# Layer 1's short chunk of a CIN tower as two fp32r passes over stacked high and low rows

## The chip, the cores and the metric

The kernel runs on one core of one Trainium2 chip. The metric is the device time of one launch in microseconds, from the program's start to its end. The core has five engines that run their own instruction streams and meet at semaphores: TensorE (PE in the profile, with its weight loads as PEld), VectorE (DVE), ScalarE (ACT), GpSimd (POOL) and SyncE (SP), which here only issues DMAs. ScalarE and GpSimd issue DMAs too.

## The reference

The model is a recommendation tower: 39 embedding tables, three cross layers (CIN), and a small MLP. For each of 1024 samples the 39 rows of 16 numbers are looked up (`x0`), and each cross layer multiplies every field of `x0` with every row of the layer before and sums the products with a filter:

```
x0 = xk = e                       # (1024, 39, 16)
for W in (f0, f1, f2):            # (39*39, 128), (128*39, 128), (128*39, 128)
    z = einsum('bfd,bgd->bfgd', x0, xk).reshape(b, f * g, d)
    cur = einsum('bpd,pm->bmd', z, W)
    outs.append(cur); xk = cur
z = sum(concatenate(outs, axis=1), axis=-1)          # (1024, 384)
h = concatenate([z, dense_ctx], axis=1)              # (1024, 400)
y = relu(relu(h @ W_top1 + b_top1) @ W_top2 + b_top2) @ W_top3
```

All inputs are fp32.

## The kernel before, in words

Columns are pairs of sample and embedding dimension, so there are 1024 x 16 of them. They are worked off in 32 groups of 512 columns (`GCOLS`), each of 4 tiles of 128 columns; 4 groups are a batch of 128 samples, and there are 8 batches. The counter `u` in the code counts tiles within a batch.

Layer 1 uses the symmetry of x0 times x0: a pair of fields is met once, by its cyclic distance. With 39 fields there are 20 distances (0 to 19). A chunk holds three distances (`SPT`), that is 117 rows (`KR`), and there are 7 chunks (`KT`): chunk k has the distances k, k+7 and k+14. Chunk 6 would have 6, 13 and 20, and since distance 20 is not needed its last 39 rows are weighted with zero. One chunk of one group is: the second factor moved into `prods[:, k]` by SyncE (`move_second`, line 272), a multiplication with the first factor in PSUM on VectorE (`multiply`, line 789), and matmuls that add into one PSUM bank (`cin1`, line 479).

A chunk is summed in one of two ways. A plain chunk (k = 0, 4, 5, 6) is one fp32 matmul, which the profile shows as two records. A split chunk (k = 1, 2, 3) has its products split: ScalarE rounds them to fp32r (`split_high`, line 654), VectorE takes what is left (`split_low`, line 795), and TensorE makes three fp32r passes: high by high, low weight by high, high weight by low.

Layer 2 is most of the work. For each tile its 39 filter slices are 10 PSUM bank loads (`BANKS`) of four slices (the last of three), each of three fp32r passes of 512 columns (lines 499, 500, 503). The banks go round a ring of 5 (`RING`): TensorE may write bank load n only when load n-5 has been read. Loads 0, 3, 5 and 7 of a tile are read by ScalarE (`scale`, line 670), loads 1, 2, 4, 6, 8 and 9 by VectorE (`mac`, line 823); both multiply by the field's scalar, and GpSimd adds up (lines 417, 421). VectorE's first sum of a tile needs ScalarE's load 0 of that tile. Layer 3 is rearranged into a small matmul per tile (line 515) and 39 per batch (line 526).

Layer 1 of the next group runs beside layer 2 of this one. The place of each of its steps is written out by hand: a pair (tile, q) in a table means "behind bank load q of that tile of the group", and each engine puts the step there in its own stream. In `PRODUCTS`, `HIGHS`, `LOWS` and `CIN1` the n-th pair is the place of the n-th product, split or chunk. In group 1 all places come three loads later (`LATE`). Group 0 runs in a prologue, all of it in fp32. SyncE works its DMAs off in order: for each group the rows to DRAM and back (lines 250, 259), first factors (266), eight moves of the scalars (326), then the second factors of the next group (272), each when `s_cin1` says that the chunk before it has been summed.

Of the kernel before, what the change touches and what calls it, by code (L numbers as in the profile page):

```python
# [26 lines left out]
F32 = mybir.dt.float32  # L27
# [6 lines left out]
P = 128  # L34
# [36 lines left out]
SPLIT = (1, 2, 3)  # L71
NS = len(SPLIT)

# [39 lines left out]
def pair_rows():  # L113

    k, i, f = np.ogrid[:KT, :SPT, :F]
    g, h = (f - KT * i) % F, (f + k) % F
    apart = KT * i + k + 0 * f
    return g * F + h, h * F + g, apart


def cin_tower(nc, dense_ctx, ids, first_row, tables, w_top1, b_top1, w_top2, b_top2, w_top3,
              w0_pair, w0_mirror, f1, f2, c_mask, c_eye, rows, out):
    with ExitStack() as ctx:
# [23 lines left out]
        prods_low = sb("prods_low", [KR, NS, GCOLS], F32R)  # L147
        x1_high = sb("x1_high", [P, 2, GCOLS], F32R)
# [16 lines left out]
        dense_rows = sb("dense_rows", [P, NBATCH, ROWS3])  # L165
# [5 lines left out]

        h1 = terms_flat[:, 0:2 * H1 // P * 512].rearrange("p (h c n) -> p h c n", h=2, c=H1 // P)
# [27 lines left out]
        s_prod = sem("products_ready")  # L200
        s_high = sem("product_highs_ready")
# [67 lines left out]
        def move_second(queue, k, j):  # L269

            at = j % GROUPS * GCOLS
            queue.dma_start(prods[0:KR, k, :], x0_cols[k:k + KR, at:at + GCOLS]).then_inc(s_second[k - 1], 16)  # L272
# [21 lines left out]
        def _(sp):  # L294
# [34 lines left out]
            def move_seconds(gf, j):  # L329

                for k in range(1, KT):
                    sp.wait_ge(s_cin1, gf * KT - KT + k + 1)
                    move_second(sp, k, j)
# [26 lines left out]
            next_cols(1, 1)  # L360
            move_seconds(1, 1)
# [89 lines left out]
        def _(pe):  # L451
# [14 lines left out]
            def cin1(gf, k, first=False):  # L466

                if k == 0:
                    pe.wait_ge(s_scal, gf + 1)
                if k in SPLIT and not first:  # L470
                    i = SPLIT.index(k)
                    pe.wait_ge(s_low, gf * NS - NS + i + 1)
                    passes = ((w0_high[:, i, :], prods_high[:, i, :]), (w0_low[:, i, :], prods_high[:, i, :]),
                              (w0_high[:, i, :], prods_low[:, i, :]))
# [3 lines left out]
                for n, (w, x) in enumerate(passes):  # L478
                    mm = nc.tensor.matmul(ps[:, X1_BANK, :], w, x, start=(k == 0 and n == 0),  # L479
                                          stop=(k == KT - 1 and n == len(passes) - 1))  # L480
# [50 lines left out]
            def prologue():  # L531
# [13 lines left out]
                for k in range(KT):  # L545
                    cin1(0, k, True)
                pe.wait_ge(s_w0h, NS)
                pe.wait_ge(s_w0l, NS)
# [370 lines left out]
```

## Time and profile before

| | before |
|---|---|
| median of 3 runs | 1282.36 us (1281.91 to 1282.44) |
| the profiled execution | 1282.15 us |
| its span, first to last instruction | 1280.3 us |
| PE busy | 1247.0 us, 97% |
| DVE busy | 1038.5 us, 81% |
| POOL busy | 951.5 us, 74% |
| ACT busy | 751.1 us, 59% |
| TensorE clock granted | 1.000 |
| DMA engines busy (queue q1 / q10) | 20.4% / 0.4% |

The busy time of an engine is the time in which any of its instructions ran. Matmuls overlap in the records: a pass of 512 columns is shown as 388 to 454 ns long, while passes start 0.23 us apart. What one costs is therefore read from the distance of starts or from the chain of work, not from the mean length. 1.85 us of the profiled execution lie outside its span.

### The profile page before, as it was taken

What the parts mean: (1) busy time and instruction counts of PE and PEld (TensorE: products, weight loads), DVE (VectorE), ACT (ScalarE), POOL (GpSimd) and SP (SyncE); (2) the same over time, 40 slices, a digit from 0 to 9 for tenths busy, and PEclk for the clock granted to TensorE, in tenths of its full rate; (3) what the DMA queues carried; (4) which work ended last, traced back from release to release, by engine and by line L of the source; (5) the groups of instructions that cost most, each with busy time, mean ns of one, the idle gap of its engine ahead of it and who ended that gap; (6) DMA issues with size and microseconds to landing.
All of it is one profiled execution on the core that took longest, in us unless ns stands there. A gap on an engine that the chain in (4) does not pass through costs nothing.

```text
span 1280.3 us, 19891 instructions
## 1 busy us (share of the span) xinstructions
PE 1247.0 (97%) x5493; PEld 963.6 (75%) x5493; DVE 1038.5 (81%) x3346; ACT 751.1 (59%) x2422; POOL 951.5 (74%) x844
## 2 busy tenths in 40 slices
PE   1999999999999999999999999999999999999999
PEld 0677778777787778777787777877787777877765
DVE  4789896898868996889969888699978898788830
ACT  4456664666646665666646666466656666466641
POOL 6578886788868886788868888588867888675640
PEclk9999999999999999999999999999999999999999
DMA  7632222122212221122221222222221222111000
GB/s 174 180 102 61 66 69 61 45 54 68 62 57 69 68 60 40 50 61 68 69 54 38 68 61 66 61 68 61 53 48 51 66 69 68 47 44 50 1 1 1
DMA packets 121764, 78.69 MB, mean 61 GB/s; under 512 B 77436, under 2 KB 89826, under 8 KB 121652
## 3 DMA queue, kind: packets, MB, share of 16 engines
q1 hardware_dynamic: 107418, 73.69, 20.4%
q0 software_dynamic: 10240, 2.64, 2.4%
q10 hardware_dynamic: 3994, 1.09, 0.4%
q8 instruction: 44, 0.72, 0.2%
q14 instruction: 68, 0.56, 0.1%
HBM read 18.50 MB, written 2.63 MB: 16 GB/s over the span
## 4 chain that ended last, share of the span: by engine, by line
PE 97%; DMA 1%; POOL 1%; issue 0%; ACTq 0%; ACT 0%; DVE 0%; SPq 0%
PE ps L499 23%; PE ps L503 22%; PE ps L500 22%; PE ps L479 14%; PE ps L526 6%; PE ps L515 5%; PE ps L582 2%; PE ps L592 1%; PE ps L462 1%; POOL x_in L393 1%; DMA x_in<-in_tables,row_at 0%; PE ps L599 0%; ACTq L272 0%; DMA x_rows<-x_in 0%; DMA ids_now<-in_ids 0%
## 5 line engine op out<-in xcount | busy, mean ns | idle before, releaser
L823 DVE SCALAR_TENSOR_TENSOR terms<-ps,x_scal,terms 128x128 f32<-128x128 f32 x2944 | 805.7, 341 | 158.4 <-ACT terms L670 94.5
L670 ACT ACTIVATE terms<-ps,x_scal 128x128 f32<-128x128 f32 x2048 | 585.3, 369 | 370.4 <-PE ps L503 363.6
L417 POOL TENSOR_TENSOR terms<-terms 128x1024 f32<-128x1024 f32 (+2 forms) x384 | 577.4, 1504 | 178.5 <-DVE terms L823 156.3
L499 PE MATMUL ps<-w_high,x_high 128*128 128x512 f32 (+1 forms) x1280 | 581.7, 454 | 2.9 <-DVE x_low L801 2.9
L503 PE MATMUL ps<-w_high,x_low 128*128 128x512 f32 (+1 forms) x1280 | 496.1, 388 | 0.0
L500 PE MATMUL ps<-w_low,x_high 128*128 128x512 f32 (+1 forms) x1280 | 494.3, 386 | 0.0
L393 POOL DMA_INDIRECT x_in<-in_tables,row_at x320 | 305.2, 954 | 81.5 <-issue 65.1
L499 PEld LDWEIGHTS ps<-w_high,x_high 128*128 128x128 f32 x1280 | 240.6, 188 | 82.9 <-issue 20.6
L500 PEld LDWEIGHTS ps<-w_low,x_high 128*128 128x128 f32 x1280 | 241.1, 188 | 77.8 <-issue 29.8
L503 PEld LDWEIGHTS ps<-w_high,x_low 128*128 128x128 f32 x1280 | 240.1, 188 | 50.5
L479 PE MATMUL ps<-prods,w 117*128 117x512 f32 x262 | 136.1, 604 | 5.2 <-DVE prods L789 5.0
L789 DVE TENSOR_TENSOR prods<-prods,ps 117x512 f32<-117x512 f32 x192 | 129.2, 674 | 1.9 <-DMA prods<-x_cols 1.9
L515 PE MATMUL ps<-x_diag,x 128*128 128x320 f32 x256 | 89.7, 432 | 0.0
L526 PEld LDWEIGHTS ps<-s,w 128*128 128x128 f32 x624 | 72.4, 192 | 4.4 <-ACT s L682 2.7
L526 PE MATMUL ps<-s,w 128*128 128x128 f32 x624 | 73.9, 276 | 0.3
L421 POOL TENSOR_TENSOR x<-terms 128x128 f32<-128x128 f32 x128 | 66.5, 520 | 10.0
L795 DVE TENSOR_TENSOR prods_low<-prods,prods_high 117x512 fp32r<-117x512 f32 x93 | 72.2, 776 | 0.0
L654 ACT ACTIVATE prods_high<-prods 117x512 fp32r<-117x512 f32 x93 | 58.7, 632 | 20.5 <-DVE prods L789 17.4
L479 PEld LDWEIGHTS ps<-prods,w 117*128 117x128 f32 x262 | 49.9, 193 | 18.4 <-issue 9.4
L682 ACT ACTIVATE s<-ps 128x320 f32<-128x320 f32 x128 | 58.1, 454 | 0.6 <-PE ps L515 0.6
L515 PEld LDWEIGHTS ps<-x_diag,x 128*128 128x128 f32 x256 | 48.2, 188 | 10.9 <-issue 0.2
L691 ACT ACTIVATE r<-ps 128x128 f32<-128x128 f32 x8 | 2.2, 279 | 67.4 <-PE ps L526 67.4
(48 smaller groups left out, 412.7 us busy)
## 6 DMA issues: line engine op xcount, KB each, us to landing
prods<-x_cols SPq DMA_DIRECT2D x189, 234.0 KB
x_cols<-x_rows SPq DMA_DIRECT2D x96, 78.0 KB
x_first<-x_cols SPq DMA_DIRECT2D x95, 78.0 KB
x_in<-in_tables,row_at POOLq DMA_INDIRECT x320
x_diag<-x_scal SPq DMA_DIRECT2D x256, 9.8 KB
x_rows<-x_in SPq DMA_DIRECT2D x32, 80.0 KB
s<-in_f SPq DMA_DIRECT2D x3, 832.0 KB, 11.6
wt<-in_W_top SPq DMA_DIRECT2D x1, 768.0 KB
```

The costliest lines, as they stand in the source:

```text
L393: pool.indirect_dma_start(out=x0_in[:, j % 2, n, :], out_offset=None, in_=tables, in_offset=bass.IndirectOffsetOnAxis(ap=row_at[:, at:at + ...
L417: nc.gpsimd.tensor_tensor(t[:, 0:n], t[:, 0:n], t[:, n:2 * n], ALU.add).then_inc(s_tree, 1)
L479: mm = nc.tensor.matmul(ps[:, X1_BANK, :], w, x, start=(k == 0 and n == 0), stop=(k == KT - 1 and n == len(passes) - 1))
L499: nc.tensor.matmul(y, x1_high[:, par, at:at + P], high, start=True, stop=False)
L500: nc.tensor.matmul(y, x1_high[:, par, at:at + P], low, start=False, stop=False)
L503: nc.tensor.matmul(y, x1_low[:, par, at:at + P], high, start=False, stop=True) \
L515: nc.tensor.matmul(ps[:, S3_BANK, 0:TB * FX], x2[:, u % 2, :], x0_diag[:, j % 2, t].rearrange("p b f -> p (b f)"), start=True, stop=True). ...
L526: mm = nc.tensor.matmul(ps[:, S3_BANK, R3_AT:R3_AT + BATCH], w2[:, f, :], s3[:, f, :], start=(f == 0), stop=(f == F - 1))
L670: op = nc.scalar.activation(terms[:, u % 2, FB * ACT_BANKS.index(q) + i, :], ps[:, (BANKS * u + q) % RING, i * G:(i + 1) * G], ACT.Copy, s ...
L789: nc.vector.tensor_tensor(prods[0:KR, k, :], second, ps[0:KR, FIRST_BANK, :], ALU.mult) \
L795: nc.vector.tensor_tensor(prods_low[:, i, :], prods[0:KR, SPLIT[i], :], prods_high[:, i, :].bitcast(F32), ALU.subtract).then_inc(s_low, 1)
L823: nc.vector.scalar_tensor_tensor(out=acc, in0=y, scalar=x0, in1=acc, op0=ALU.mult, op1=ALU.add).then_inc(s_mac, 1)
```

## The change

The chunk with only two distances (6 and 13, 78 rows, `KH`) becomes number 1 in the order of the chunks (`SHIFT_OF`, `REST`). It is no longer summed in fp32 but in two fp32r passes of 117 rows. `rest` holds the high parts of its 78 rows, and in its last 39 rows the low parts of one of the two distances; `w0_rest` holds the matching weights:

- pass 0: high weights on the high rows, and the high weights of distance 6 on the low rows of distance 6;
- pass 1: low weights on the high rows, and the high weights of distance 13 on the low rows of distance 13.

The 39 low rows are written by VectorE to `prods_low` on other partitions than those at which they are needed, so each pass has a DMA before it from `prods_low` to `rest[78:117]`. ScalarE issues both (`move_rest`, at the places `MOVE_LOWS`); the second waits until pass 0 has read the rows. The chunks of distances from 1, 2 and 3 on are still split in three passes, now under the numbers 2, 3 and 4; plain chunks are 0, 5 and 6. The third split product moves forward from (2,3) to (2,1), with its high part at (2,2) and low part at (2,3). `dense_rows` now lies in `r2`, which makes room for the new tiles. In the prologue the weights of the chunk are split and two DMAs on SyncE copy their high rows; group 0 sums the chunk in fp32, in two halves of 256 columns, so that it too fills two of the 8 places.

```diff
-SPLIT = (1, 2, 3)
+SHIFT_OF = (0, KT - 1) + tuple(range(1, KT - 1))
+REST, SPLIT = 1, (2, 3, 4)
 NS = len(SPLIT)
+KH = (SPT - 1) * F
...
-PRODUCTS = ((0, 2), (0, 4), (1, 2), (1, 7), (2, 3), (2, 5), (2, 7))
-HIGHS = ((0, 6), (1, 4), (1, 8))
-LOWS = ((0, 7), (1, 5), (1, 9))
-CIN1 = ((0, 6), (1, 1), (1, 8), (2, 6), (2, 9), (3, 2), (3, 4))
+PRODUCTS = ((0, 2), (0, 4), (1, 2), (1, 7), (2, 1), (2, 5), (2, 7))
+HIGHS = ((0, 6), (1, 4), (1, 8), (2, 2))
+LOWS = ((0, 7), (1, 5), (1, 9), (2, 3))
+MOVE_LOWS = ((0, 8), (1, 3))
+CIN1 = ((0, 6), (1, 3), (1, 8), (2, 1), (2, 6), (2, 9), (3, 2), (3, 4))
+CIN1_OF = (0, REST, 2, REST, 3, 4, 5, 6)
...
+        def move_rest(queue, i):
+
+            queue.dma_start(rest[KH:KR, :].bitcast(F32), prods_low[i * F:(i + 1) * F, 0, :].bitcast(F32)) \
+                .then_inc(s_rest, 16)
...
             next_cols(1, 1)
+            sp.wait_ge(s_w0l, 1)
+            for i in range(2):
+                sp.dma_start(w0_rest[KH:KR, i, :].bitcast(F32), w0_rest[i * F:(i + 1) * F, 0, :].bitcast(F32)) \
+                    .then_inc(s_wrest, 16)
             move_seconds(1, 1)
...
+                elif k == REST:
+                    pe.wait_ge(s_wrest, 32)
+                    pe.wait_ge(s_rest, (gf - 1) * 32 + half * 16 + 16)
+                    passes = ((w0_rest[:, half, :], rest[:, :]),)
...
+                if k == REST:
+                    act.wait_ge(s_cin1, (gf - 1) * SLOTS + REST_SLOTS[1] + 1)
+                    nc.scalar.activation(rest[0:KH, :], prods[0:KH, k, :], ACT.Copy).then_inc(s_high, 1)
...
+                    if front and now == MOVE_LOWS[0]:
+                        act.wait_ge(s_low, (gf - 1) * (NS + 1) + 1)
+                        move_rest(act, 0)
+                    if front and now == MOVE_LOWS[1]:
+                        act.wait_ge(s_cin1, gf * SLOTS + REST_SLOTS[0] + 1)
+                        move_rest(act, 1)
...
+                if k == REST:
+                    if gf > 1:
+                        dve.wait_ge(s_cin1, (gf - 2) * SLOTS + SLOTS + CIN1_OF.index(SPLIT[-1]) + 1)
+                    nc.vector.tensor_tensor(prods_low[0:KH, 0, :], prods[0:KH, k, :],
+                                            rest[0:KH, :].bitcast(F32), ALU.subtract).then_inc(s_low, 1)
+                else:
+                    if i == NS:
+                        dve.wait_ge(s_rest, gf * 32)
```

The new order is seen best at three places. The first is TensorE's stream in the second tile of a group, bank loads 1 to 3 (`w1_high` and `x1_high` are layer 2; `w0_high` is layer 1). Before:

```order
452 L499 MATMUL ps<-w1_high,x1_high 128x512
453 L500 MATMUL ps<-w1_low,x1_high 128x512
454 L503 MATMUL ps<-w1_high,x1_low 128x512
455 L479 MATMUL ps<-prods_high,w0_high 128x512
456 L479 MATMUL ps<-prods_high,w0_low 128x512
457 L479 MATMUL ps<-prods_low,w0_high 128x512
458 L499 MATMUL ps<-w1_high,x1_high 128x512
459 L500 MATMUL ps<-w1_low,x1_high 128x512
460 L503 MATMUL ps<-w1_high,x1_low 128x512
```

In the changed kernel the same stretch, from bank load 2 on:

```order
462 L532 MATMUL ps<-w1_high,x1_high 128x512
463 L533 MATMUL ps<-w1_low,x1_high 128x512
464 L536 MATMUL ps<-w1_high,x1_low 128x512
465 L532 MATMUL ps<-w1_high,x1_high 128x512
466 L533 MATMUL ps<-w1_low,x1_high 128x512
467 L536 MATMUL ps<-w1_high,x1_low 128x512
468 L512 MATMUL ps<-rest,w0_rest 128x512
```

The three layer-1 passes behind bank load 1 are gone from there, and one pass over `rest` stands behind bank load 3.

The second place is ScalarE's stream from the last bank load of a group's first tile (load 7) to the split of the second tile. Before:

```order
255 L670 ACTIVATE terms<-ps,x0_scal 128x128 [waits y_bank_ready]
256 L670 ACTIVATE terms<-ps,x0_scal 128x128 x3
257 L670 ACTIVATE terms<-ps,x0_scal 128x128 [waits y_bank_ready,x2_ready]
258 L670 ACTIVATE terms<-ps,x0_scal 128x128 x3
259 L670 ACTIVATE terms<-ps,x0_scal 128x128 [waits y_bank_ready]
260 L670 ACTIVATE terms<-ps,x0_scal 128x128 x3
261 L654 ACTIVATE prods_high<-prods 117x512 [waits products_ready]
```

In the changed kernel:

```order
271 L708 ACTIVATE terms<-ps,x0_scal 128x128 [waits y_bank_ready]
272 L708 ACTIVATE terms<-ps,x0_scal 128x128 x3
273 L288 DMA rest<-prods_low 39x512 [waits product_lows_ready]
274 L708 ACTIVATE terms<-ps,x0_scal 128x128 [waits y_bank_ready,x2_ready]
275 L708 ACTIVATE terms<-ps,x0_scal 128x128 x3
276 L708 ACTIVATE terms<-ps,x0_scal 128x128 [waits y_bank_ready]
277 L708 ACTIVATE terms<-ps,x0_scal 128x128 x3
278 L288 DMA rest<-prods_low 39x512 [waits x1_chunks_summed]
279 L692 ACTIVATE prods_high<-prods 117x512 [waits products_ready]
```

A DMA issue now stands before load 0 of the second tile, and another between load 3 and the split.

The third place is VectorE's stream in the third tile of a group. Before:

```order
120 L823 SCALAR_TENSOR_TENSOR terms<-ps,x0_scal,terms 128x128 [waits macs_done,y_bank_ready]
121 L823 SCALAR_TENSOR_TENSOR terms<-ps,x0_scal,terms 128x128 [waits macs_done] x3
122 L789 TENSOR_TENSOR prods<-prods,ps 117x512 [waits second_factor_moved4]
123 L823 SCALAR_TENSOR_TENSOR terms<-ps,x0_scal,terms 128x128 [waits macs_done,y_bank_ready]
124 L823 SCALAR_TENSOR_TENSOR terms<-ps,x0_scal,terms 128x128 [waits macs_done] x3
125 L789 TENSOR_TENSOR prods<-prods,ps 117x512 [waits second_factor_moved5]
```

In the changed kernel the product of chunk 4 is one place further up, and a split follows:

```order
121 L834 TENSOR_TENSOR prods<-prods,ps 117x512 [waits second_factor_moved4]
122 L877 SCALAR_TENSOR_TENSOR terms<-ps,x0_scal,terms 128x128 [waits macs_done,y_bank_ready]
123 L877 SCALAR_TENSOR_TENSOR terms<-ps,x0_scal,terms 128x128 [waits macs_done] x3
124 L849 TENSOR_TENSOR prods_low<-prods,prods_high 117x512 [waits rest_lows_moved,product_highs_ready]
125 L877 SCALAR_TENSOR_TENSOR terms<-ps,x0_scal,terms 128x128 [waits macs_done,y_bank_ready]
126 L877 SCALAR_TENSOR_TENSOR terms<-ps,x0_scal,terms 128x128 [waits macs_done] x3
127 L834 TENSOR_TENSOR prods<-prods,ps 117x512 [waits second_factor_moved5]
```

VectorE thus has one more instruction per group, and it stands in the third tile; its length and what waits for it are to be read from the trace.

## Rows read from the trace of the kernel before

**Rows 1.** Parts 1 and 4 of the page, busy time and last chain:

```profile
PE 1247.0 (97%) x5493; PEld 963.6 (75%) x5493; DVE 1038.5 (81%) x3346; ACT 751.1 (59%) x2422; POOL 951.5 (74%) x844
...
PE 97%; DMA 1%; POOL 1%; issue 0%; ACTq 0%; ACT 0%; DVE 0%; SPq 0%
```

**Rows 2.** Window (length; busy PE, PEld, DVE, ACT, POOL; clock; DMA; GB/s), PE's longest wait:

```profile
45.00:1228.00 1183.00, 1181.14 (x5273) 928.37 (x5272) 1015.07 (x3304) 723.03 (x2368) 916.64 (x805) 1.00 0.23 60
...
PE ps L499 <- DVE x_low L801: 1.4, 1, 1.4
```

**Rows 3.** Chain in order of time (start, us, what) around one group's start:

```profile
534.09 0.86 PE ps L479 x2
...
538.25 0.70 PE ps L479 x3
```

**Rows 4.** Group of line 479 by form, the plain chunks:

```profile
L479 PE MATMUL ps<-prods,w 117*128 117x512 f32 x262 | 136.1, 604 | 5.2 <-DVE prods L789 5.0 <-ACT x_scal L640 0.2
```

**Rows 5.** Timeline of PE: second tile's start, its chunk, load 4, third tile:

```profile
536.69 0.40 PE L499 MATMUL ps<-w_high,x_high 128*128 128x512 f32 x1
...
538.08 0.40 PE L479 MATMUL ps<-prods_high,w_high 117*128 117x512 f32 x1
...
540.17 0.39 PE L499 MATMUL ps<-w_high,x_high 128*128 128x512 f32 x1
...
545.38 0.40 PE L499 MATMUL ps<-w_high,x_high 128*128 128x512 f32 x1
```

**Rows 6.** Timeline of ACT: loads 7 and 0, then the split at (1,4):

```profile
535.69 1.14 ACT L670 ACTIVATE terms<-ps,x_scal 128x128 f32<-128x128 f32 x4 [0.54 <-PE ps L503]
537.65 1.15 ACT L670 ACTIVATE terms<-ps,x_scal 128x128 f32<-128x128 f32 x4 [0.81 <-PE ps L503]
...
541.61 0.63 ACT L654 ACTIVATE prods_high<-prods 117x512 fp32r<-117x512 f32 x1
```

**Rows 7.** Timeline of SP, DMA issues of one group:

```profile
539.83 0.39 SPq L250 DMA_DIRECT2D x_rows<-x_in  x1
542.22 1.49 SPq L259 DMA_DIRECT2D x_cols<-x_rows  x4
545.12 2.40 SPq L266 DMA_DIRECT2D x_first<-x_cols  x3
```

**Rows 8.** Windows around those transfers, columns as in rows 2:

```profile
544.50:545.10 0.60, 0.60 (x5) 0.51 (x4) 0.60 (x3) 0.51 (x3) 0.60 (x1) 1.00 0.00 0
...
545.10:546.50 1.40, 1.40 (x8) 1.22 (x7) 1.40 (x7) 0.59 (x2) 1.18 (x3) 1.00 0.00 0
546.50:547.10 0.60, 0.60 (x4) 0.47 (x4) 0.60 (x2) 0.60 (x3) 0.36 (x1) 1.00 0.48 133
```

**Rows 9.** ScalarE's DMA issues of lines 266 and 272, ns min/median/max:

```profile
L266 ACTq DMA_DIRECT2D x_first<-x_cols x1: 1405/1405/1405, 24.6 to 24.6; - x1
...
L272 ACTq DMA_DIRECT2D prods<-x_cols x3: 793/811/865, 26.1 to 27.7; - x3
```

**Rows 10.** Timeline of DVE: first split, second tile's start and end, third tile:

```profile
535.44 0.68 DVE L795 TENSOR_TENSOR prods_low<-prods,prods_high 117x512 fp32r<-117x512 f32 x1
...
538.82 2.16 DVE L823 SCALAR_TENSOR_TENSOR terms<-ps,x_scal,terms 128x128 f32<-128x128 f32 x8 [0.56 <-ACT terms L670]
...
546.61 0.67 DVE L795 TENSOR_TENSOR prods_low<-prods,prods_high 117x512 fp32r<-117x512 f32 x1
547.52 2.16 DVE L823 SCALAR_TENSOR_TENSOR terms<-ps,x_scal,terms 128x128 f32<-128x128 f32 x8 [0.24 <-ACT terms L670]
```

**Rows 11.** Timeline near the start: ACT's weight split, SP in group 1 and 2, DVE:

```profile
23.90 0.69 ACT L710 ACTIVATE w_high<-w 117x128 fp32r<-117x128 f32 x3
...
64.07 0.43 SPq L250 DMA_DIRECT2D x_rows<-x_in  x1
...
80.32 4.99 SPq L272 DMA_DIRECT2D prods<-x_cols  x6
...
83.76 0.69 DVE L789 TENSOR_TENSOR prods<-prods,ps 117x512 f32<-117x512 f32 x1 [0.34 <-DMA prods<-x_cols]
```

More of the change, by code:

```diff
@@ L147, in cin_tower @@
         prods_low = sb("prods_low", [KR, NS, GCOLS], F32R)
+        rest = sb("rest", [KR, GCOLS], F32R)
+        w0_rest = sb("w0_rest", [KR, 2, G], F32R)
         x1_high = sb("x1_high", [P, 2, GCOLS], F32R)
@@ L271, in move_second @@
             at = j % GROUPS * GCOLS
-            queue.dma_start(prods[0:KR, k, :], x0_cols[k:k + KR, at:at + GCOLS]).then_inc(s_second[k - 1], 16)
+            row, n = SHIFT_OF[k], KH if k == REST else KR
+            queue.dma_start(prods[0:n, k, :], x0_cols[row:row + n, at:at + GCOLS]).then_inc(s_second[k - 1], 16)
+        def move_rest(queue, i):
+            queue.dma_start(rest[KH:KR, :].bitcast(F32), prods_low[i * F:(i + 1) * F, 0, :].bitcast(F32)) \
+                .then_inc(s_rest, 16)
         def prologue_then_batches(eng, step, prologue, tail):
@@ L329, in move_seconds @@
             def move_seconds(gf, j):
-                for k in range(1, KT):
-                    sp.wait_ge(s_cin1, gf * KT - KT + k + 1)
-                    move_second(sp, k, j)
+                for n in range(1, SLOTS):
+                    sp.wait_ge(s_cin1, gf * SLOTS - SLOTS + n + 1)
+                    if n != REST_SLOTS[0 if gf == 1 else 1]:
+                        move_second(sp, CIN1_OF[n], j)
             def next_cols(gf, j):
@@ L477, in cin1 @@
                     passes = ((w0[:, k, :], prods[0:KR, k, :]),)
-                for n, (w, x) in enumerate(passes):
-                    mm = nc.tensor.matmul(ps[:, X1_BANK, :], w, x, start=(k == 0 and n == 0),
-                                          stop=(k == KT - 1 and n == len(passes) - 1))
+                for i, (w, x) in enumerate(passes):
+                    mm = nc.tensor.matmul(ps[:, X1_BANK, cols], w, x, start=(k == 0 and i == 0),
+                                          stop=(n == SLOTS - 1 and i == len(passes) - 1))
                 mm.then_inc(s_cin1, 1)
@@ L544, in prologue @@
                 pe.wait_ge(s_denl, len(DENSE_BANKS))
[L545 to L548, printed above, removed]
+                for n in range(SLOTS):
+                    cin1(0, n, True)
+                pe.wait_ge(s_w0h, NS + 1)
+                pe.wait_ge(s_w0l, NS + 1)
                 pe.wait_ge(s_w1h, len(W1_PIECES))
@@ L708, in prologue @@
                 act.wait_ge(s_w0s, 1)
+                nc.scalar.activation(w0_rest[0:KH, 0, :], w0[0:KH, REST, :], ACT.Copy).then_inc(s_w0h, 1)
                 for i, k in enumerate(SPLIT):
```

47 lines of the change are left out of this document (32 added, 15 removed).

## The prediction

> **What bounds the kernel now.** I read the busy shares and the chain that ended last first [rows 1]: TensorE is busy 97% of the span and is 97% of the chain, while VectorE is at 81%. An average can hide stages with another limit, so the second view is one window over the steady part. From 45 to 1228 us TensorE is busy 1181.14 of 1183 us, at full granted clock, and the longest wait in it is a single one of 1.4 us [rows 2]. So TensorE's stream is the time there. An edit gains what it takes out of that stream, and loses what it makes the stream wait; no other engine's busy time counts until its lateness reaches TensorE. The third view is the chain in order of time, which gives what one chunk costs in the stream: a plain fp32 chunk 0.86 us, a split chunk of three fp32r passes 0.70 us, so 0.23 us a pass [rows 3]. The mean length of 604 ns [rows 4] is no price: its 262 records are 131 chunks of two records each (31 groups with four, 7 in group 0), and they overlap.
>
> **What TensorE's stream loses.** In each of the 31 groups after group 0 one plain chunk of 0.86 us becomes two passes of 0.23 us: 0.86 - 0.46 = 0.40 us. Times 31 that is 12.4 us. The other chunks are only renumbered. The size of this term hardly depends on anything else, because a pass over `rest` has the rows, columns and form of the passes in rows 3.
>
> **The first move of low rows.** This is the one new wait with little room. Before, the split chunk (1,1) needed only what VectorE had written. Now pass 0 at (1,3) needs a DMA that ScalarE issues behind its reading of load 7. I put the change's order on the times of the group at 528 us. VectorE's split ends at 535.44 + 0.68 = 536.12 [rows 10]; ScalarE's reading of load 7 ends at 535.69 + 1.14 = 536.83 [rows 6], so ScalarE does not wait for VectorE, and the issue starts at about 536.83. TensorE begins load 4 at 540.17 [rows 5], which in the old order has the three passes of 0.70 us before it; without them load 3 ends at 539.47, and there pass 0 is due. The room is 539.47 - 536.83 = 2.64 us.
>
> How long such a move takes from issue to landing is not shown for this queue, so I bound it. The lower end is the nearest whole round trip of about 80 KB: SyncE issues `x_rows` at 539.83 and, having waited for it, goes on at 542.22 [rows 7], 2.39 us. The upper end is a second factor: issued at 80.32, used by a waiting VectorE at 83.76 [rows 11], 3.44 us, but that carries 117 rows instead of 39 and stands in a busy start. In between lies the transfer most like it, the first factor's 39 rows from SBUF to SBUF: issued at 545.12, no traffic until 546.5, and 0.6 us at 133 GB/s, which is its 80 KB, until 547.1 [rows 7, 8]. To that comes the time from the last byte to the waiting engine, for which `x_cols` stands: no traffic after 544.50, SyncE goes on at 545.12, 0.62 us. The sum is 1.98 + 0.62 = 2.60 us, against 2.64 us of room. I take this as the value, and a wait of 0.07 us a group, since the wait stands before the pass's weight load too and so wants the semaphore somewhat before 539.47: 31 x 0.07 = 2.2 us. The bounds are 0 (at 2.39) and 0.80 us a group (at 3.44), 25 us in all.
>
> The Trainium skill ("DMA: Bandwidth & Descriptors", Anatomy of one DMA) fits a DMA as about 2.0 us plus its bytes over 436 GB/s, on another issue path. For 80 KB that would be 2.18 us and no wait at all. It also says that most of the fixed part is the receipt of the write; by rows 7 and 8 here 1.4 us pass before the first byte and 0.62 us after the last, so the trace differs on where the time lies.
>
> **ScalarE.** It gains a high split and two issues per group. Its issues took 0.79 to 0.87 us, the very first 1.41 [rows 9]. The first stands between load 7 and load 0: that gap is 537.65 - 536.83 = 0.82 us [rows 6], so it just fits. The second stands between load 3 and the split at (1,4). TensorE ends load 3 there 0.70 us earlier than before, so ScalarE reaches the issue 0.70 us earlier and is done about when it began that split, 541.61 [rows 6]. I cost both at nothing; the cover is these two gaps. The second move has from about 541 until (2,1), some 5 us, against at most 3.44. The new high split at (2,2) holds ScalarE back until VectorE's product at (2,1), about 549 to 549.6, though load 3 of that tile was ready at 548; TensorE wants that bank again at load 8, near 551.9, and ScalarE has read it by 550.8. Nothing as well.
>
> **VectorE.** It gains one instruction a group, 0.6 to 0.7 us by rows 10; products and splits of 78 rows are priced like those of 117, since the trace has none of 78. What counts is the tightest place. In the second tile VectorE has no gap from 538.82 to 547.28 [rows 10], while TensorE now starts the third tile at 545.38 - 0.70 + 0.23 = 544.91 [rows 5]. VectorE therefore enters the third tile at 547.28, not after a gap at 547.52, and has the product and now a split in it. Following its stream, at 1.04 us a load (two of them in the 2.16 us of rows 10) and 0.6 for a product, load 2 of the third tile is read at 547.28 + 1.04 + 0.6 + 1.04 = 549.96. TensorE needs that bank for load 7. A load is three passes, 0.69; line 515's pass is what remains of the second tile's 8.69 us [rows 5] after ten loads (6.73) and two chunks (1.40), 0.56. So load 7 begins at 544.91 + 7 x 0.69 + 0.23 + 0.56 + 0.70 = 551.2. 1.2 us of room are left, and in the fourth tile, where two plain chunks of 0.86 us slow TensorE, VectorE catches up. Cost nothing; if ScalarE's first issue is late by 0.5 us this room shrinks by as much and still holds.
>
> **The start.** The chain there runs over ScalarE, which has one more small activation, about 0.2 us by 0.69 for three [rows 11]. SyncE gets two more moves. It was busy without pause up to its `x_rows` issue at 64.07, and the lateness goes on to the second factors at 80.32, for which VectorE already waited 0.34 us at 83.76 [rows 11]. Two issues cost 1.2 to 1.6 us (0.8 each at 2.40 for three [rows 7]); the move is smaller now, and I take 1.0 us that reaches TensorE, between 0 and 1.6. Group 0's two halves have the same columns as one whole.
>
> **Sum.** -12.4 + 2.2 + 0.2 + 1.0 = -9.0 us. Against the profiled execution's own 1282.15 us this is 1273.2 us. That execution lies 0.2 us under the median of 1282.36, inside the spread of the runs.
>
> **Rivals.**
> - *The moves land in time.* Landing takes 2.39 us and not 2.60, and the start's lateness is taken up by the ring: 1282.15 - 12.4 + 0.2, about 1270.0 us. The round trip of `x_rows` speaks for it; against it, the issue alone of an SBUF to SBUF move is 0.8 us and not 0.39 [rows 7]. The skill's page above leads to the same case.
> - *VectorE or the ring binds in the second and third tile.* The new split and ScalarE's delayed readings use up the 1.2 us. TensorE would wait 0.1 to 0.2 us a group at a layer 2 pass: 3 to 6 us more, 1276 to 1279 us. For it: no gap of VectorE in the second tile [rows 10]. Against it: the fourth tile gives everything back, so lateness does not add up over groups.
> - *The first move comes late, and the kernel is slower.* Place: pass 0 at (1,3). If ScalarE's issue costs 1.41 us each time, as its first did [rows 9], or the landing takes 3.44 us, TensorE waits 0.6 to 0.8 us in each of 31 groups. The price is 19 to 25 us against a gain of 12.4, so about 1290 to 1296 us. It decides from a wait of 0.36 us a group on, which is (12.4 - 1.2) / 31: a landing later than 3.0 us after the issue. Against it: the other three issues of ScalarE took 0.8, and in the steady part the DMA engines are busy 23% [rows 2].
> - *The change doesn't do what it says*: two passes of mixed rows cost the stream as much as the fp32 chunk. Each would have to take 0.43 us instead of 0.23; nothing in rows 3 speaks for it.
>
> **Chances.** Forecast (a wait of up to 0.2 us a group) 0.42; moves in time 0.27; ring or VectorE 0.15; late and slower 0.09; a wait that eats the gain almost exactly, or no gain, 0.07. Less than 0.2% either way, 2.6 us, is about what a measurement of this kernel cannot tell from no change. The first three cases are faster, with small parts at the edge: faster 0.85, same 0.06, slower 0.09. The range goes from the case without any wait or start term, 1269.6, to the upper end of the ring's case, 1279.3; beyond it lies mainly the slower rival. The forecast's own range is 1271 to 1277.
>
> **What would show it.** In the new trace: 0.46 us for the two `rest` passes in the chain and plain records going from 262 to 202 (31 groups with three chunks and 8 in group 0, two records each) would show the gain. A group should take about 0.33 to 0.40 us less. TensorE's waits before the pass over `rest` at (1,3), put down to the DMA, should be some 0.1 us each; none, and it is the first rival; 0.4 or more, and the forecast is wrong. ScalarE's issues should last near 0.8 us and load 0 of the second tile be read no later than before. VectorE's wait for a second factor in group 2 should grow to 1 us or more. Waits of layer 2 passes for VectorE or ScalarE in the third tile would show the second rival.

## The result and the profile after

| | before | after |
|---|---|---|
| median of 20 runs each, us | 1282.19 (1281.20 to 1283.11) | 1284.06 (1282.09 to 1285.74) |
| profiled execution, us | 1282.15 | 1285.17 |
| its span, us | 1280.3 | 1283.4 |

The ratio of after to before is 1.0015, with a 95% interval of 1.0009 to 1.0022. In place of the predicted gain of 9 us (to 1273.2 us, range 1269.6 to 1279.3) the change costs 1.9 us. The prediction is wrong.

First the page of the changed kernel, parts 1 and 4, answering to [rows 1]:

```profile
PE 1240.8 (97%) x5495; PEld 962.5 (75%) x5495; DVE 1070.5 (83%) x3378; ACT 757.5 (59%) x2454; POOL 960.5 (75%) x844
...
PE 74%; DVE 14%; ACT 3%; SPq 3%; issue 2%; DMA 2%; POOL 1%; ACTq 0%
PE ps L532 17%; PE ps L536 17%; PE ps L533 16%; PE ps L512 10%; DVE terms L877 9%; PE ps L559 6%; PE ps L548 4%; DVE prods_low L849 3%; DVE prods L834 2%; ACT terms L708 2%; PE ps L615 2%; POOL x_in L415 1%; PE ps L625 1%; PE ps L484 1%; SPq L329 1%
```

TensorE's busy time fell by 6.2 us, so work did leave it. But the chain is no longer TensorE alone: a quarter of it now runs over other engines, mostly VectorE. The busy shares hide this, since VectorE only went from 81% to 83%.

Next, in the changed kernel, the window that answers to [rows 2] with the same columns, and TensorE's waits that were not there before or grew (us in total, times, longest):

```profile
45.00:1228.00 1183.00, 1172.97 (x5258) 924.51 (x5257) 1044.40 (x3326) 726.78 (x2389) 922.93 (x802) 1.00 0.24 63
```

```profile
PE ps L559 <- ACT s L720: 3.5, 7, 0.6
PE ps L512 <- DMA rest<-prods_low: 3.0, 2, 2.0
...
PE ps L532 <- DVE terms L877: 0.8, 1, 0.8
```

TensorE now stands idle for 10.0 of these 1183 us, before for 1.9. The first row belongs to the end of each batch. The other two belong to the start: the wait for VectorE is at 88.92 us, in group 2. The time that VectorE costs in the steady part isn't in these rows, since it only spreads passes apart whose records overlap.

The work that was removed is really gone. These pieces of the chain in order of time (start, us, what) and groups of line 512 answer to [rows 3] and [rows 4]:

```profile
366.50 0.23 PE ps L512
```

```profile
L512 PE MATMUL ps<-prods,w 117*128 117x512 f32 x202 | 103.3, 598 | 5.2 <-DVE prods L834 5.0
```

```profile
L512 PE MATMUL ps<-rest,w_rest 117*128 117x512 f32 x62 | 24.9, 402 | 3.0 <-DMA rest<-prods_low 3.0
```

The pass over `rest` takes 0.23 us of the stream, and the plain records went from 262 to 202, both as predicted.

Where the time went is easiest to see by following one event that occurs once a batch: the first piece of layer 3's per-batch matmuls in the chain. The pieces before (line 526), second batch to last:

```profile
199.14 3.14 PE ps L526 x26
...
349.25 3.17 PE ps L526 x26
...
1099.92 3.17 PE ps L526 x26
```

The same after (line 559):

```profile
204.78 3.14 PE ps L559 x26
...
354.21 3.17 PE ps L559 x26
...
1102.92 3.17 PE ps L559 x26
```

Before, a batch of four groups took (1099.92 - 199.14) / 6 = 150.13 us; after, (1102.92 - 204.78) / 6 = 149.69 us. That is a gain of 0.44 us a batch where 4 x 0.40 = 1.6 was expected. On top, the first of these events comes 5.6 us late instead of 1.6 us early (groups 1 to 4 lie ahead of it). So of the 12.4 us that were to be gained, 7.2 us are lost ahead of 204.78, 6 x 1.16 = 7.0 us in the six batches, and the remaining 1.3 us in the last three groups (the span grew by 3.1: 7.2 + 7.0 + 1.3 - 12.4). The steady part and the start have different causes.

**Steady part, VectorE.** A stretch of VectorE's and GpSimd's timelines in the changed kernel (start, us, engine, line, operation), third tile of the group at 420 us, answering to [rows 10]:

```profile
428.68 2.16 DVE L877 SCALAR_TENSOR_TENSOR terms<-ps,x_scal,terms 128x128 f32<-128x128 f32 x8 [0.55 <-ACT terms L708]
...
432.39 1.12 DVE L849 TENSOR_TENSOR prods_low<-prods,prods_high 117x512 fp32r<-117x512 f32 x1
...
436.88 0.68 DVE L849 TENSOR_TENSOR prods_low<-prods,prods_high 117x512 fp32r<-117x512 f32 x1
...
438.51 0.67 DVE L834 TENSOR_TENSOR prods<-prods,ps 117x512 f32<-117x512 f32 x1
...
440.14 1.59 DVE L849 TENSOR_TENSOR prods_low<-prods,prods_high 117x512 fp32r<-117x512 f32 x1
441.65 1.11 DVE L877 SCALAR_TENSOR_TENSOR terms<-ps,x_scal,terms 128x128 f32<-128x128 f32 x4
```

```profile
439.89 1.30 POOL L439 TENSOR_TENSOR terms<-terms 128x512 f32<-128x512 f32 x1
441.26 1.06 POOL L439 TENSOR_TENSOR terms<-terms 128x256 f32<-128x256 f32 x1
```

The same instruction takes 0.68 us at 436.88 and 1.59 us at 440.14. In the second case GpSimd is in the middle of its sums (line 439): the one over 128x512 began at 439.89 and ends at 441.19. The split ends at 441.73, which is 0.54 us after that. The chain runs over VectorE from 428.68 to 442.78 without a gap, and TensorE takes it back here (timeline of PE, the last load of the third tile):

```profile
442.34 0.40 PE L536 MATMUL ps<-w_high,x_low 128*128 128x512 f32 x1
442.82 0.44 PE L532 MATMUL ps<-w_high,x_high 128*128 128x384 f32 x1
```

A pass usually follows the one before after 0.23 us; this one follows after 0.48. Load 9 wanted the bank of load 4, which VectorE read until 442.76. So in this group 0.25 us were lost at this one place alone.

Summed over the kernel, the 93 splits of line 849 are busy 89.2 us and the 93 of line 795 before were 72.2:

```profile
L849 DVE TENSOR_TENSOR prods_low<-prods,prods_high 117x512 fp32r<-117x512 f32 x93 | 89.2, 959 | 0.0
```

```profile
L795 DVE TENSOR_TENSOR prods_low<-prods,prods_high 117x512 fp32r<-117x512 f32 x93 | 72.2, 776 | 0.0
```

The mean of 776 ns before says that some of the old splits were stretched too. The timelines of the whole kernel show which. Before, those at (0,7) and (1,9) took 0.68 us in every group, and those at (1,5) 0.97 us in the mean (25 of 31 were stretched, the longest to 1.27). After, those at (1,5) took 0.93 in the mean and the new ones at (2,3) 1.27 (23 of 31 stretched, the longest to 1.60). I priced the new one from two rows of 0.68 and 0.67 us [rows 10] and did not look at the mean.

**The end of each batch.** The row `PE ps L559 <- ACT s L720` above is this: with a shorter stream TensorE reaches the per-batch matmuls before ScalarE has stored the last sums, seven times, 0.5 us each in the mean.

**The start.** In the changed kernel, timeline of DVE, ACTq and PE in group 2, answering to [rows 11]:

```profile
87.15 0.68 DVE L834 TENSOR_TENSOR prods<-prods,ps 78x512 f32<-78x512 f32 x1 [2.67 <-DMA prods<-x_cols]
...
89.50 0.77 ACTq L288 DMA_DIRECT2D rest<-prods_low  x1
...
93.52 0.76 PE L512 MATMUL ps<-rest,w_rest 117*128 117x512 f32 x1 [2.00 <-DMA rest<-prods_low]
94.08 0.63 PE L532 MATMUL ps<-w_high,x_high 128*128 128x512 f32 x1
94.51 0.63 PE L533 MATMUL ps<-w_low,x_high 128*128 128x512 f32 x1
```

SyncE is late with the second factors (VectorE waits 2.67 us; before it was 0.34), and then TensorE waits 2.00 us for the small move: 4.0 us from its issue to its use, in a stretch where the DMA engines are busy 41% of the time (the window below). After that wait passes follow at 0.43 us and not at 0.23. The window rows of the two kernels, before and then after, show it as a granted clock of 0.83:

```profile
90.00:100.00 10.00, 10.00 (x45) 8.16 (x44) 10.00 (x31) 7.86 (x26) 9.18 (x8) 1.00 0.27 61
```

```profile
90.00:100.00 10.00, 8.00 (x28) 5.81 (x27) 7.76 (x26) 5.60 (x19) 6.42 (x7) 0.83 0.41 107
```

### The profile page after: what moved, and what is told of

Same layout as the page of the kernel before. It is cut to its first block, busy times and chain, and to the rows that moved or that the text cites. A ratio compares the mean times of both kernels' runs of the same rounds, so it can differ in the third digit from the quotient of the medians.

```text
span 1283.4 us, 20208 instructions
## 1 busy us (share of the span) xinstructions
PE 1240.8 (97%) x5495; PEld 962.5 (75%) x5495; DVE 1070.5 (83%) x3378; ACT 757.5 (59%) x2454; POOL 960.5 (75%) x844
## 3 DMA queue, kind: packets, MB, share of 16 engines
q0 software_dynamic: 10240, 2.64, 2.3%
## 4 chain that ended last, share of the span: by engine, by line
PE 74%; DVE 14%; ACT 3%; SPq 3%; issue 2%; DMA 2%; POOL 1%; ACTq 0%
PE ps L532 17%; PE ps L536 17%; PE ps L533 16%; PE ps L512 10%; DVE terms L877 9%; PE ps L559 6%; PE ps L548 4%; DVE prods_low L849 3%; DVE prods L834 2%; ACT terms L708 2%; PE ps L615 2%; POOL x_in L415 1%; PE ps L625 1%; PE ps L484 1%; SPq L329 1%
## 5 line engine op out<-in xcount | busy, mean ns | idle before, releaser
L439 POOL TENSOR_TENSOR terms<-terms 128x1024 f32<-128x1024 f32 (+2 forms) x384 | 586.5, 1527 | 170.8 <-DVE terms L877 131.4
L532 PE MATMUL ps<-w_high,x_high 128*128 128x512 f32 (+1 forms) x1280 | 571.6, 447 | 4.6 <-DVE x_low L855 2.9
L834 DVE TENSOR_TENSOR prods<-prods,ps 117x512 f32<-117x512 f32 (+1 forms) x192 | 129.3, 675 | 4.0 <-DMA prods<-x_cols 4.0
L512 PE MATMUL ps<-prods,w 117*128 117x512 f32 x202 | 103.3, 598 | 5.2 <-DVE prods L834 5.0
L849 DVE TENSOR_TENSOR prods_low<-prods,prods_high 117x512 fp32r<-117x512 f32 x93 | 89.2, 959 | 0.0
L559 PEld LDWEIGHTS ps<-s,w 128*128 128x128 f32 x624 | 72.4, 192 | 7.6 <-ACT s L720 5.5
L559 PE MATMUL ps<-s,w 128*128 128x128 f32 x624 | 73.9, 276 | 3.5 <-ACT s L720 3.5
L720 ACT ACTIVATE s<-ps 128x320 f32<-128x320 f32 x128 | 59.1, 461 | 0.6 <-PE ps L548 0.6
L512 PEld LDWEIGHTS ps<-prods,w 117*128 117x128 f32 x202 | 38.9, 194 | 17.0 <-issue 7.6
```

What stands on the lines that cost most here:

```text
L439: nc.gpsimd.tensor_tensor(t[:, 0:n], t[:, 0:n], t[:, n:2 * n], ALU.add).then_inc(s_tree, 1)
L512: mm = nc.tensor.matmul(ps[:, X1_BANK, cols], w, x, start=(k == 0 and i == 0), stop=(n == SLOTS - 1 and i == len(passes) - 1))
L532: nc.tensor.matmul(y, x1_high[:, par, at:at + P], high, start=True, stop=False)
L559: mm = nc.tensor.matmul(ps[:, S3_BANK, R3_AT:R3_AT + BATCH], w2[:, f, :], s3[:, f, :], start=(f == 0), stop=(f == F - 1))
L834: nc.vector.tensor_tensor(prods[0:n, k, :], second, ps[0:n, FIRST_BANK, :], ALU.mult) \
L849: nc.vector.tensor_tensor(prods_low[:, i % NS, :], prods[0:KR, k, :], prods_high[:, i - 1, :].bitcast(F32), ALU.subtract).then_inc(s_low, 1)
```

## The experiments

Ratios are to the kernel before, run on the same chip in the same set, with 95% intervals. "Batch" and "first event" are read as above.

### Four kernels that take the two suspected causes apart

`e1_weights_early` issues the two moves of the weights' low rows earlier in SyncE's stream:

```diff
-            put(sp, 0, 1)
-            load_cols(sp, 1, 1)
-            next_cols(1, 1)
             ... (the two w0_rest moves)
+            put(sp, 0, 1)
+            load_cols(sp, 1, 1)
+            next_cols(1, 1)
```

> The changed kernel with SyncE's two moves of the chunk's weight rows issued before the second group's rows instead of behind its first factors, when SyncE has nothing else to do. Theory S (part of the lost gain is at the start: SyncE is late by 4 us at the second factors of group 2, TensorE waits 2.0 us for the move of low rows there and then runs for some us at a lower clock): the wait of VectorE at group 2 falls from 2.7 us to about 1, TensorE's wait for the low rows to under 1 us, no fall of the granted clock at 90 to 100 us, and the time falls by 2 to 4 us to about 1281; steady batches stay at 149.4 to 149.9 us. Rival (the lateness comes from the slower weight loads, not from the two moves): within 1 us of the changed kernel.

Measured: 1283.10 us, 1.0010 (1.0001 to 1.0019). Batch 149.9, first event 203.39. VectorE's wait for the product of group 2 fell from 2.67 to 1.2 us, but TensorE still waited 2.06 us for the small move, and the clock was again 0.83 from 90 to 100 us. The gain of 2 to 4 us that the theory wanted did not come. The changed kernel itself, profiled once more (`a1`, below), had its first event at 202.98, so this run alone proves nothing about the start.

`e2_split_later` puts both halves of the new split behind load 7 and 8 of the third tile, and sums chunk 4 one slot later:

```diff
-HIGHS = ((0, 6), (1, 4), (1, 8), (2, 2))
-LOWS = ((0, 7), (1, 5), (1, 9), (2, 3))
+HIGHS = ((0, 6), (1, 4), (1, 8), (2, 7))
+LOWS = ((0, 7), (1, 5), (1, 9), (2, 8))
-CIN1_OF = (0, REST, 2, REST, 3, 4, 5, 6)
+CIN1_OF = (0, REST, 2, REST, 3, 5, 4, 6)
```

> The changed kernel with the third three-pass split at (2,7) on ScalarE and (2,8) on VectorE instead of (2,2) and (2,3); its passes stand at (3,2), and the plain chunk 5 takes (2,9). Theory G (a subtraction on VectorE with both sources in SBUF takes 1.0 to 1.6 us where GpSimd's sums run, and 0.68 where they do not; at (2,3) it always meets them, and VectorE becomes late for TensorE's ring): line 849's mean falls from 959 to about 800 ns, a batch takes about 148.5 us instead of 149.7, and the time falls by 8 to 9 us to about 1275.5. Rival M (the two moves issued by ScalarE, or the passes over rest, cost the time): no change of the batch, within 1 us of the changed kernel.

Measured: 1278.75 us, 0.9978 (0.9969 to 0.9987). Batch 149.04: the direction came, with about half of the size that I had expected (148.5). Its splits:

```profile
L849 DVE TENSOR_TENSOR prods_low<-prods,prods_high 117x512 fp32r<-117x512 f32 x93 | 72.2, 776 | 0.0
```

The 17 us of stretching are gone, and with them 0.65 us a batch.

Its start is worth a look too. In this profile VectorE waits longer for the late second factor, TensorE then waits 2.08 us for VectorE to free a bank, and the passes behind that are slow already, before the small move is due (timelines of DVE and PE, then a window):

```profile
86.76 0.68 DVE L834 TENSOR_TENSOR prods<-prods,ps 78x512 f32<-78x512 f32 x1 [3.94 <-DMA prods<-x_cols]
88.53 0.51 PE L532 MATMUL ps<-w_high,x_high 128*128 128x512 f32 x1 [2.08 <-DVE terms L877]
```

```profile
90.00:92.50 2.50, 2.29 (x6) 1.29 (x4) 2.23 (x10) 1.30 (x5) 1.66 (x2) 0.50 0.90 233
```

`e3_small_sums` leaves the order as it is and lets GpSimd's tree of sums work on 8 of 128 columns; it leaves out the other 120 columns of those sums:

```diff
-nc.gpsimd.tensor_tensor(t[:, 0:n], t[:, 0:n], t[:, n:2 * n], ALU.add).then_inc(s_tree, 1)
+nc.gpsimd.tensor_tensor(t[:, 0:n, 0:8], t[:, 0:n, 0:8], t[:, n:2 * n, 0:8], ALU.add).then_inc(s_tree, 1)
```

> The changed kernel with GpSimd's sums over 8 of the 128 columns only (the three halving sums of terms); the rest is left out. Theory G: the subtractions all take 0.68 us, VectorE is never late in the third tile, a batch takes 148.5 us or a little less, the time about 1275. Rival O (VectorE is late because of the order alone: ScalarE is held at (2,2) until the product is there, and VectorE has one instruction too many in two tiles): the subtractions may get shorter, but batches stay at 149.4 us or more and the time above 1281.

Measured: 1278.83 us, 0.9977 (0.9967 to 0.9986). Batch 149.12, where 148.5 or a little less was expected. The 0.6 us that this and the run before fall short turn up below, at the end of the batch.

```profile
L849 DVE TENSOR_TENSOR prods_low<-prods,prods_high 117x512 fp32r<-117x512 f32 x93 | 63.2, 680 | 0.0
```

The split stands where the change put it, yet all 93 now take 680 ns, the slowest of them 685. So it is GpSimd's work that stretches it, and not its place as such. Two different edits that have in common only that the split does not meet the sums give the same batch.

`e4_both` has the edits of `e1` and `e2`.

> Both edits, the weight rows moved early and the third split later. If the two losses are separate, their gains add up: 2 to 4 us from the start and 8 to 9 us from the steady part, about 1272 us, which is 0.8% under the kernel before. If only one of the theories holds, the time is that of the one run alone.

Measured: 1276.30 us, 0.9959 (0.9945 to 0.9973). Batch 149.02, first event 200.54. TensorE's longest wait for the move is 1.1 us, and the clock from 90 to 100 us is 1.00. The time that I had expected, 1272 us, was not reached, since the steady part gave only half. At the start the two edits together give more than each alone: the first event is at 204.78, 203.39, 202.28 and 200.54 in after, `e1`, `e2` and `e4`. The prologue's length varies from profile to profile, so the distance from the first pass of layer 2 says more: 163.7, 162.4, 161.7 and 158.7 us, against 158.0 before. The same distance is 161.4 in the changed kernel's second profile (`a1`), 163.1 in `e5` and 159.5 in `e3`. Of the kernels with GpSimd's full sums only `e4` is clearly shorter. `e4` is `e2` with the weights' moves earlier, and 2.45 us faster in the median. With the split out of the way, then, SyncE's lateness does cost time; the profile of `e2` shows how.

### Which half of the split matters

Moving both halves in `e2` left a rival: that it was ScalarE, held at its high split until VectorE's product is there, that read its bank late. `e5_low_only_later` moves only the low split and leaves the high one at (2,2):

```diff
-LOWS = ((0, 7), (1, 5), (1, 9), (2, 3))
+LOWS = ((0, 7), (1, 5), (1, 9), (2, 8))
-CIN1_OF = (0, REST, 2, REST, 3, 4, 5, 6)
+CIN1_OF = (0, REST, 2, REST, 3, 5, 4, 6)
```

> The changed kernel with only VectorE's half of the third split moved, from (2,3) to (2,8); ScalarE's half stays at (2,2), where ScalarE waits for the product, and the passes stand at (3,2). Theory G (the meeting with GpSimd's sums at (2,3) is what costs): the subtraction is down to 0.68 us, a batch takes 149.05 us as in the run with both halves moved, about 1278.8 us. Rival O (ScalarE held at (2,2) costs the ring): batches stay at 149.5 us or more, about 1283.

Measured: 1277.95 us, 0.9970 (0.9959 to 0.9981). Batch 149.05, with ScalarE still waiting 102.0 us in all at its high splits:

```profile
L692 ACT ACTIVATE prods_high<-prods 117x512 fp32r<-117x512 f32 x93 | 58.8, 632 | 104.4 <-DVE prods L834 102.0 <-PE ps L512 2.5
L849 DVE TENSOR_TENSOR prods_low<-prods,prods_high 117x512 fp32r<-117x512 f32 x93 | 72.5, 779 | 0.0
```

The same batch as with both moved, where ScalarE waited only 40.6 us in all at these splits. Its waiting costs nothing, as predicted, and the rival falls.

### The small move and the traffic around it

`e6_late_loads` is `e4` with the loads of the later weights (`wt`, `bt`) issued one group later, so that they are out of group 2:

```diff
-            load_late()
             ...
+                if j == 2:
+                    load_late()
```

> The kernel with both edits (1276.3 us), and the loads of the later weights (3.3 MB) moved on SyncE from before the feed of group 2 to behind that of group 3. Theory S (the start loses because the second factors, and the move of low rows with them, are issued 4 us late behind those loads, and the low rows then share the DMA engines with the second factors): no wait of TensorE for the low rows in group 2, the first batch ends 2 to 4 us earlier than 200.5 us, about 1273 us. Rival: the wait only moves to a later group, where the loads now meet the feed, and the time stays within 1 us of 1276.3.

`b1_before_late_loads` makes the same edit in the kernel before.

> The kernel before, with the loads of the later weights moved in the same way and nothing else. It tells how much of that edit's gain has nothing to do with the two passes. TensorE of the kernel before waits little at the start (18.6 of 20 us busy from 60 to 80 us), so 0 to 2 us faster, 1280 to 1282 us; if the start's loss belonged to the old kernel as much as to the new, it would gain the same 3 us.

Measured: `e6` 1278.68 us, 0.9973 (0.9963 to 0.9983), no better than `e4`'s 0.9959 (0.9945 to 0.9973), and far from the 1273 us that I had expected. `b1` 1281.59 us, 0.9994 (0.9985 to 1.0003), no different from before. In `e6` the stretch from 45 to 100 us is as clean as it was before the change (TensorE 53.23 us busy, before 53.40). But group 3 now has the collision: the move waits for the traffic (timeline, ACTq and PE), and the clock falls again (window of 20 us):

```profile
120.80 0.80 ACTq L288 DMA_DIRECT2D rest<-prods_low  x1
...
127.40 0.47 PE L513 MATMUL ps<-rest,w_rest 117*128 117x512 f32 x1 [3.13 <-DMA rest<-prods_low]
```

```profile
120.00:140.00 20.00, 16.87 (x68) 13.34 (x67) 14.60 (x48) 10.41 (x35) 13.17 (x12) 0.91 0.47 125
```

In `b1` the same stretch has the same transfers and no wait:

```profile
120.00:140.00 20.00, 20.00 (x88) 16.16 (x87) 18.78 (x61) 12.58 (x43) 16.73 (x16) 1.00 0.42 109
```

So the traffic alone costs nothing. This loss needs the new move on TensorE's path, and it went where the traffic went.

### The end of the batch, the best version, and two controls

`e7_batch_end` is `e6` with layer 3's per-batch matmuls in two parts behind loads 8 and 9, in place of three:

```diff
-CIN3 = (7, 8, 9)
+CIN3 = (8, 9)
```

> As the run before, and layer 3's 39 matmuls per batch in two parts behind loads 8 and 9 of the last tile instead of three behind 7, 8 and 9. Theory: of the 0.40 us a group that the passes save, 0.13 is given back at the end of a batch, where TensorE now reaches those matmuls before ScalarE has stored the last sums (0.5 us a batch); one load later the wait is gone and a batch takes 148.6 us instead of 149.05, 3 to 4 us in all. Rival: the longer parts starve ScalarE and VectorE and the gain is under 1 us.

Measured: 1274.35 us, 0.9940 (0.9926 to 0.9953). Batch 148.37, 0.68 less than in `e6`.

`e8_both_and_batch_end` has that edit on `e4`, without the moved loads.

> The kernel of e4 (weights' low rows moved early, low split of chunk 4 at (2,8)) with layer 3's per-batch matmuls in two parts behind loads 8 and 9 in place of three behind 7, 8 and 9. Theory: three causes ate the gain, and this takes away all three. In e7 against e6 the same step took 0.70 us off a batch (149.05 to 148.35), so seven steady batches give 4.9 us: 1276.3 - 4.9, about 1271.4 us at the start of e4 (first batch at 200.5). Rival: the shorter batch end only hands its time to the next wait (VectorE or ScalarE in the first tile of the next batch), and the time is 1274 or more.

Measured: 1271.63 us (1271.17 to 1274.08), 0.9931 (0.9918 to 0.9945), as expected. First event 201.05, batch (1091.26 - 201.05) / 6 = 148.37. The part 4 of its page:

```profile
PE 93%; SPq 3%; DMA 2%; POOL 1%; issue 1%; ACT 0%; DVE 0%
```

VectorE and ScalarE are out of the chain. From 100 to 1228 us TensorE has no idle record:

```profile
100.00:1228.00 1128.00, 1128.00 (x5085) 893.08 (x5084) 986.45 (x3186) 705.19 (x2294) 884.35 (x776) 1.00 0.22 59
```

`b2_before_batch_end` makes only that edit, in the kernel before.

> The kernel before with layer 3's per-batch matmuls in two parts behind loads 8 and 9, nothing else. Theory: in the kernel before TensorE waits only about 0.03 to 0.07 us a batch (2.7 us for 6 weight loads in part 5) for ScalarE's last sums, since its stream is longer; so the batch stays near 150.13 us and the time within 0.5 us of before. Rival: the three-part form itself costs TensorE something in either kernel (each part restarts the chain of small matmuls, which e7's pieces of 4.24 + 4.46 against 3.17 + 2.90 + 2.90 show as 0.27 us less in all), and this kernel gains 0.3 to 0.7 us a batch, 2 to 5 us in all.

Measured: 1280.24 us, 0.9987 (0.9978 to 0.9996). Batch 149.86 against 150.13. Neither line was quite met. The batch falls by 0.27 us though TensorE hardly waited there before; it is the form. In three parts these matmuls are pieces of 3.17 + 2.90 + 2.90 = 8.97 us of the chain, in two parts 4.24 + 4.46 = 8.70. So of the 0.68 us of `e7`, 0.27 are to be had in the kernel before as well, and 0.41 are the wait that the shorter stream had brought up.

`a1_after_again` is the changed kernel once more, beside these two.

> The changed kernel once more, beside the two above on the same chip. Theory: ratio 1.001 to 1.002 to the kernel before, with a batch of 149.7 us and a first batch at 204 to 205. Rival: the slight loss was that of one chip or one set of runs, and it now stands at 0.999 or less.

Measured: 1283.82 us, 1.0018 (1.0008 to 1.0027), with a batch of 149.85 and the first event at 202.98. The slight loss is real. The start differs by 1.8 us between two profiles of the same kernel: here TensorE waited 1.3 us at most for the move, and the clock of the stretch from 45 to 100 us was 1.00, in the other profile 0.97.

## Why the prediction was wrong, step by step

**What TensorE's stream loses: right.** 0.23 us a pass, 60 plain records fewer. Cleanest is `e8` against `b2`, which have the same batch end: 149.86 - 148.37 = 1.49 us a batch, 0.37 a group where I had 0.40.

**The first move's wait: wrong in size for the steady part, wrong in place.** I had 0.07 us in each of 31 groups, 2.2 us in all. In the steady part there is none; that 3.0 us of such waits came together at the start is chance, not this term. I let ScalarE issue the move only when its reading of load 7 had ended. The new trace shows the issue running while that reading still does (timeline of ACT and ACTq, answering to [rows 6] and [rows 9]):

```profile
390.63 0.62 ACT L708 ACTIVATE terms<-ps,x_scal 128x128 f32<-128x128 f32 x2 [0.54 <-PE ps L536]
391.09 0.79 ACTq L288 DMA_DIRECT2D rest<-prods_low  x1
391.15 0.62 ACT L708 ACTIVATE terms<-ps,x_scal 128x128 f32<-128x128 f32 x2
...
394.39 0.40 PE L512 MATMUL ps<-rest,w_rest 117*128 117x512 f32 x1
```

It starts 0.03 us after VectorE's low split ends (391.06) and 0.68 us before the reading ends (391.77), so the room is 3.3 us and not 2.64. The move does decide something, but in groups where other transfers run.

**ScalarE: right.** 62 issues of 774 to 812 ns; `e5` shows that its waiting at the new high split costs nothing.

**VectorE: this is the step that failed in the steady part.** "Cost nothing", from one new instruction of 0.6 to 0.7 us against 1.2 us of room in the third tile. The rival on VectorE had the place, the direction and the size (0.1 to 0.2 us a group): after against `e5` is 149.69 - 149.05 = 0.64 us a batch, 0.16 a group. With the batches of `a1` and `e1`, whose steady part is the same as after's (149.85 and 149.87), it is up to 0.82, or 0.2 a group.

Three things were wrong in that step. The instruction was mis-sized: 1.27 us in the mean at (2,3), up to 1.60 where GpSimd is at its sums. The working also stopped too early: it followed VectorE to load 2, whose bank load 7 wants, but the new split stands behind that, ahead of load 4, whose bank load 9 wants. Carried on with my own numbers, load 4 is read at 549.96 + 0.68 + 1.04 = 551.7 and load 9 begins at 551.2 + 2 x 0.69 = 552.6, so the room was 0.9 us and not 1.2; with 1.60 in place of 0.68 it is gone. And the group I read was a mild one: its split at (1,5) took 0.71 us, where 0.97 is the mean, so in most groups VectorE enters the third tile later than I had it. `e3` shows the cause of the stretching.

The Trainium skill ("SBUF — State Buffer", Who interferes with whom) has this rule: a VectorE instruction with two inputs in SBUF contends with a GpSimd instruction that reads SBUF, and one with at most one such input doesn't. It calls the shared ports an exclusive lock, so that the later instruction stands until the earlier has ended. The trace agrees: the low splits, whose inputs are both in SBUF, are stretched up to 1.60 us; the products, which take one input from PSUM, stayed at 0.67 in the same stretch (438.51). By an exclusive lock the split at 440.14 would start to read when the sum ends at 441.19 and end by 441.87; it ended at 441.73, 0.14 us sooner, so the rule holds here only roughly. This rule spoke against the change, and I had not weighed it.

**The batch's end: not in the sum at all.** I looked for what is late next only around layer 1. TensorE's next appointment outside it, with ScalarE's last stored sums, cost 0.41 us a batch.

**The start: the term of 1.0 us was too small, and for another reason than given.** The loss up to the first event is 7.2 us, in the second profile of the same kernel 5.4. Of the 7.2, 4.0 us are more idle time of TensorE from 45 to 100 us (5.58 against 1.60), and about 1.7 us (0.17 of 10 us, an estimate) are the lower clock that followed. The remaining 1.5 us I can't place; they aren't in the prologue, since layer 2 begins at 41.04 us and before at 41.11. In this profile the larger part of the idle time is the small move that meets other transfers: 3.0 us of waits (0.99 in group 1, 2.00 in group 2). The 0.8 us of waiting for VectorE stand behind its wait for SyncE's late second factors, which I had priced, and are gone in `e1` and `e4`; in the profile of `e2` that wait is 2.08 us and the move's 0.94. How the loss divides between the two thus changes from execution to execution, and no run takes the move away alone. I had bounded the move for the steady groups and used that for the first ones too; even its upper end of 3.44 us was too short there.

**The six batches together:** expected 1.6 us each; less 0.64 for VectorE, less 0.41 for the batch's end, makes 0.55, and 0.44 was measured. The missing 0.1 us agrees with the 0.03 us a group that `e8` against `b2` leaves open. I don't know its cause, and profiles with the same steady part differ by as much (149.69 to 149.87). What is left of the start's loss in `e8` also stays: TensorE is 50.79 us busy from 45 to 100 us against 53.40 in `b2`, and waits 1.3 us for a move. Whether a quieter place for it exists was not tried.

The rivals: the one on VectorE and the ring did occur, with its size, but I had it alone, and not together with a costly start. The slower rival named the right cause for the start, the move's landing, but for 31 groups, and it occurred in two. The low end of my range is a slip in the sum: 1282.15 - 12.4 is 1269.75 and not 1269.6, which changes nothing here. The chance of 0.85 for faster was far too high: the covers of VectorE, of the move, of SyncE and of what comes next had all to hold at once, and I priced each as if it held for certain.

## What to carry to other kernels

Before an instruction is added to an engine at a price from one row, compare the mean of its group with that row; a mean well above it says that some neighbour stretches it, and the new place may be next to that neighbour. When TensorE's stream gets shorter, walk the whole period and list every appointment it will now reach earlier, not only those near the edit. A small transfer put on the critical path has no fixed length: bound it in the busiest stretch in which it will run, above all at the start.

## What the hardware showed that I had not expected

- A subtraction of 117x512 with both inputs in SBUF takes 0.68 us alone and up to 1.60 us beside GpSimd's sums over SBUF (once 2.28 us, in `e2` at 68.66, where the sum beside it is the one over 128x1024). With the small sums of `e3` all 93 are within 675 to 685 ns.
- A move of 39 rows (80 KB) from SBUF to SBUF was in time in every group of the steady part, with 3.3 us from issue to use in the one at 390 us. In one busy stretch it was used only 4.0 us after its issue and in another 6.6 us after it, with TensorE waiting.
- ScalarE's DMA issue runs while its activation still does: the issue starts at 391.09 us, the reading of load 7 ends at 391.77.
- After waits of 2.0 and 3.1 us near the start, TensorE's granted clock was 0.83 and 0.91 in the stretches that followed (of its levels of 2.4 and 1.2 GHz, passes then follow at 0.43 us, the lower one). It isn't the move as such that does it: in `e2` the clock fell behind the 2.08 us for a bank of VectorE's. In `e4` and `a1`, with waits of 1.1 and 1.3 us at most, it stayed at 1.00.
- The same 39 small matmuls (78 records) cost 8.97 us in three parts and 8.70 in two.
